# One wait between a batch's row stores, and the exponential of the memory weights moved behind the values' copies

## The chip, the cores and the metric

The kernel runs on one core of a Trainium2 chip. A core has five engines that run their own instruction streams and meet at semaphores: TensorE (PE, matrix products), VectorE (DVE), ScalarE (ACT), GpSimd (POOL) and SyncE (SP, which issues DMAs). The metric is the device time of one execution in microseconds (us), the median of several.

## The reference

A block of a network on 4 sequences of 1024 rows with 256 columns, in float32: a layer norm, then the sum of the input, an attention part and a part of experts.

```python
xn = layernorm(x)
x = x + attention(xn) + ffn(xn)

# attention, 16 heads of 16 columns, 4 memories
sq, sk = elu(q) + 1, elu(k) + 1
a_f, n_f = einsum(sq, memories), einsum(sq, memory_norms)
rel = n_f.mean(-1)                     # per batch and head: mean over the 1024 rows
w = softmax(rel, axis=0)               # over the 4 memories: the "memory weights"
out_fine = ((a_f / clip(n_f, EPS)) * w).sum(0)
memory_output = p * out_fine + (1 - p) * out_coarse      # p from a small gate network
local_output = causal_linear_attention(q, k, v)
attention = (gate * memory_output + (1 - gate) * local_output) @ w_o.T

# ffn: softmax over 8 experts, the best 2 of each row, plus a shared expert
g = silu(xn @ w_gate[e]) * (xn @ w_up[e]);  y += cw[row, e] * (g @ w_down[e])
y += silu(xn @ sw_gate) * (xn @ sw_up) @ sw_down
```

## The kernel before

The program has three phases, one after the other.

**Tokens phase** (the first 186 us or so). It is unrolled over the four batches, which the code counts as b = 2, 3, 4, 5, and two buffers u = 0, 1 alternate. For each batch DVE takes the mean and variance of the rows (meanvar, lines 572 and 577), POOL makes rstd and shift of them (varp, rstd, shift, lines 801 to 804, function scale_and_shift), ACT normalizes the rows into xn (line 447), PE transposes them in two halves (t_a, line 311), ACT and DVE copy the transposes as a high and a low part, xT (lines 463 and 669), and PE multiplies them with the shared expert's weights (t_g and t_u, and then the down product t_y; each product is three matmuls, lines 87 to 89). DVE adds t_y to the rows (xn_in, line 697), and SP stores that. Each batch is 8 tiles of 128 rows. From the logits DVE computes where each row goes, slot_i, and POOL then stores every row twice (TOP = 2), once for each chosen expert, to the place in d_rows: 16 indirect DMAs of 128 rows, 128 KB each (line 821). Each adds 16 to a semaphore s_sc[u] when it has landed. Around the end of a batch these stores run while PE does the down product of the second half, the transposes of the next batch's second half, and its first products. SP then loads the batch after that and a quarter of the experts' weights.

**Experts phase** (to about 360 us). SP loads blocks of 128 rows of one expert from d_rows, and PE, ACT and DVE run the experts on them.

**Attention phase** (the rest). All engines walk one list, ATT_ORDER, made by attention_order(); an item is (what, batch, tile, part), and each engine does those items that are its own, in the list's order, and waits on semaphores for the others'. So an item's place in the list sets its place in an engine's queue, even where its data are ready earlier or later. A batch has 8 tiles, t = 0 to 7. What matters here:

- "norms": PE multiplies sq with the memories; ACT copies it to with_mem (line 1554), four copies for a tile.
- "mean" (t = 0): PE gives the mean of n_f over the batch; DVE copies it to mw and subtracts the maximum (lines 1644 to 1648).
- "mexp" (t = 0): ACT takes the exponential of mw (line 1526).
- "weights": DVE sums and divides, five small instructions on mw (lines 1654 to 1661).
- "values": PE multiplies the masked scores (probs) with v (line 1452); ACT copies the result to valT, two copies (line 1574); PE multiplies these with a picking matrix in "local" (line 1474), and DVE divides (den, line 1687, to mem_rows, line 1690).
- "state" and "fold": the running sum of keys and values on PE (line 1497) and its copy on DVE (line 1712).
- "coef": DVE makes the coefficients from the gate's e_t, from rn and from mw (lines 1695 to 1698). It is the first reader of mw after "weights", in the list of the next tile.
- "scores": PE's scores (line 1417) and DVE's masking, probs (line 1681).

Of the kernel before, what the change touches and what calls it, by code (L numbers as in the profile page):

```python
# [36 lines left out]
TS = ST // P  # L37
# [72 lines left out]
def tokens_phase(nc, d, c, w):  # L110

    with ExitStack() as scope:
# [677 lines left out]
        def _(pool):  # L790
# [17 lines left out]
            for it in range(B // 2):  # L808
                for u in range(2):
                    b = it * 2 + (2 + u)  # L810
                    if b == 2:
                        scale_and_shift(3)

                    pool.wait_ge(s_slot, b + 1)
                    pool.wait_ge(c["s_load"], (c["n_load"] - 1) * 16)
                    pool.wait_ge(s_tick, b)
                    pool.tensor_tensor(tick_p[:, :], c["lane"][:, :], c["lane"][:, :],
                                       ALU.add).then_inc(s_tick, 1)
                    for t in range(NT):
                        for k in range(TOP):  # L820
                            pool.indirect_dma_start(  # L821
                                d["rows"], bass.IndirectOffsetOnAxis(ap=slot_i[u][:, k, t:t + 1], axis=0),
                                xn[u][:, t, :], None).then_inc(s_sc[u], 16)
                    if b < B:
                        scale_and_shift(b + 2)
# [270 lines left out]
def attention_order():  # L1096
    def parts(items, engine):
        return [(what + engine, *at) for what, *at in items if what in ON_TWO]
# [7 lines left out]
    for i, (b, t) in enumerate(tiles):  # L1106
# [16 lines left out]
        order += [("scores", b, t, j) for j in range(4)]  # L1123
        if i > 1:
            order.append(("outT", *tiles[i - 2], 0))
        if i:
            order += [("coef", *tiles[i - 1], 0), ("rest", *tiles[i - 1], 0)]
        order.append(("coarseT", b, t, 0))
# [12 lines left out]
        if i + 1 < len(tiles):  # L1141
            order += [("norms", *tiles[i + 1], j) for j in range(NB3)]
        if t == 0:
            order += [("mean", b, 0, 0), ("mexp", b, 0, 0)]
        order += ahead + [("values", b, t, 0), ("values", b, t, 1)] + behind + [("gate", b, t, 0)]
        projected = parts(ahead + behind, ".dve")
        rows = [x for x in projected if x[0] == "xT.dve"]
        late = [x for x in projected if x[0] != "xT.dve"]
        order += parts(ahead + behind, ".act")
        if t < NT - 1:  # L1150
            order.append(("state", b, t, 1))
        if t == 0:
            order.append(("weights", b, 0, 0))
        order += rows
        if t < NT - 1:
            order.append(("fold", b, t, 1))
# [24 lines left out]
def attention_phase(nc, d, c, w):  # L1181

    with ExitStack() as scope:
# [400 lines left out]
        def _(dve):  # L1584
# [17 lines left out]
            def walk(items):  # L1602
                link, _ = chain(dve, s_dve)
                for item in items:
# [45 lines left out]
                                          ALU.subtract).then_inc(s_mx, 1)  # L1650
                    elif what == "weights":

                        since(dve, s_mexp, b + 1)
                        link(dve.tensor_reduce(mw_m[:, 0, :, :], by_memory, AX.X, ALU.add))
                        link(dve.reciprocal(mw_m[:, 1, :, :], mw_m[:, 0, :, :]))
# [232 lines left out]
```

## Time and profile before

| | |
|---|---|
| median of 3 runs | 712.3 us |
| their lowest and highest | 708.75, 714.91 us |
| the profiled execution | 708.62 us |
| its span, first to last instruction | 706.7 us |
| mean granted TensorE clock | 0.956 of full speed |
| PE busy | 626.9 us (89%) |
| DVE busy | 509.9 us (72%) |
| ACT busy | 355.9 us (50%) |
| POOL busy | 313.4 us (44%) |

Busy times are sums over the span; an engine that is idle in one phase can be the one that all wait for in another. The profile was taken of one execution. An engine's row ends with the idle time just before it and what ended that, in square brackets; "issue" is a time for which the profile shows no wait, and "remote" one whose release it cannot match to an instruction. The ends of PE's instructions are modelled, and some of its records can be missing.

### The profile page before, as it was taken

To read this page: it belongs to the slowest core of one execution; us is meant where nothing else is said; L and a number is where in the kernel's file an instruction comes from. 1 tells how busy PE (TensorE), PEld (TensorE's weight loads), DVE (VectorE), ACT (ScalarE), POOL (GpSimd) and SP (SyncE) were. 2 spreads that over 40 slices of the span, in tenths; PEclk is the share of its full clock that TensorE was granted. 3 is DMA by queue.
4 is the path that set the end of the run, shared out by engine and by line. 5 is a ranking of instruction groups with operands and counts; after the bars stand their busy time and mean duration, and the time that the engine had idled before them with its cause. 6 is when DMAs were issued, how large, how long until landed. Compare 5 with 4: busy or idle time off the path is not lost. (4 is left out here: it accounts for less than half of the span.)

```text
span 706.7 us, 22451 instructions
## 1 busy us (share of the span) xinstructions
PE 626.9 (89%) x7874; PEld 520.5 (74%) x7874; DVE 509.9 (72%) x1362; ACT 355.9 (50%) x902; POOL 313.4 (44%) x406
## 2 busy tenths in 40 slices
PE   1997869699499999999968999989998999989885
PEld 0785748578399999999956777777776777777663
DVE  3674829358466666666656988889888788888886
ACT  4453625252434444444435766556565475646542
POOL 1153543707481000000030766656675566666775
PEclk9999989989599999999978999999999999999996
DMA  8128271534353333333350012221140202103120
GB/s 283 64 91 277 78 257 56 189 136 149 121 167 116 117 120 118 121 114 117 116 183 34 18 33 92 84 85 32 36 137 29 84 25 65 60 17 92 33 63 32
DMA packets 60123, 71.39 MB, mean 101 GB/s; under 512 B 7612, under 2 KB 55068, under 8 KB 60028
## 3 DMA queue, kind: packets, MB, share of 16 engines
q1 hardware_dynamic: 50956, 52.61, 22.9%
q0 software_dynamic: 6656, 16.86, 7.3%
q8 instruction: 67, 1.10, 0.7%
q10 hardware_dynamic: 2416, 0.59, 0.4%
q14 instruction: 28, 0.23, 0.1%
HBM read 38.45 MB, written 31.59 MB: 99 GB/s over the span
## 5 line engine op out<-in xcount | busy, mean ns | idle before, releaser
L1741 POOL TENSOR_TENSOR tick_a<-lane 128x1 f32<-128x1 f32 x32 | 6.3, 196 | 148.1 <-POOLq L834 145.8
L1744 POOL DMA_INDIRECT yg<-d_grouped_y,from_row x64 | 62.5, 977 | 15.5 <-issue 11.6
L978 ACT ACTIVATE hb<-e_h 88x256 fp32r<-88x256 f32 x72 | 27.5, 382 | 52.7 <-PE e_h L953 52.7
L87 PE MATMUL e_up<-wb,xb 128*128 x144 | 53.0, 368 | 0.5 <-issue 0.5
L1554 ACT ACTIVATE with_mem<-a_ring 128x340 f32<-128x340 f32 x128 | 47.0, 450 | 7.8 <-PE a_ring L1398 7.5
L1010 DVE TENSOR_TENSOR h_sb<-e_up,silu 128x176 f32<-128x176 f32 x72 | 24.6, 342 | 35.3 <-ACT silu L973 35.3
L87 PE MATMUL e_y<-wd,hb 88*128 x146 | 48.7, 334 | 1.0 <-DVE hb L1017 1.0
L1769 POOL TENSOR_TENSOR mem_rows<-mem_rows 128x512 f32<-128x512 f32 x16 | 24.3, 1518 | 54.5 <-DVE mem_rows L1721 54.5
L1681 DVE TENSOR_TENSOR probs<-a_ring,causal 128x256 f32<-128x256 f32 x128 | 45.1, 415 | 3.5 <-remote 3.3
L89 PE MATMUL e_up<-wb,xb 128*128 x144 | 46.9, 326 | 0.0
L88 PE MATMUL e_up<-wb,xb 128*128 x144 | 46.9, 326 | 0.0
L973 ACT ACTIVATE silu<-e_up 128x176 f32<-128x176 f32 x72 | 22.9, 318 | 41.1 <-PE e_up L89 41.1
L1474 PE MATMUL a_ring<-ident,valT 128*128 128x68 f32 x256 | 35.3, 279 | 8.4 <-ACT valT L1574 8.4
L88 PE MATMUL e_y<-wd,hb 88*128 x146 | 41.6, 285 | 0.0
L1474 PEld LDWEIGHTS a_ring<-ident,valT 128*128 128x128 f32 x256 | 31.0, 191 | 14.2 <-issue 11.0
L89 PE MATMUL e_y<-wd,hb 88*128 x146 | 41.3, 283 | 0.0
L1017 DVE TENSOR_TENSOR hb<-e_h,hb 88x256 fp32r<-88x256 f32 x72 | 30.3, 420 | 14.7 <-ACT hb L978 12.5
L821 POOL DMA_INDIRECT d_rows<-v,slot_i x32 | 34.0, 1063 | 9.5 <-issue 9.5
L821 POOL DMA_INDIRECT d_rows<-sqT,slot_i x32 | 33.0, 1032 | 9.5 <-issue 9.5
L1430 PE MATMUL a_ring<-wo,attT 128*128 128x256 f32 x128 | 35.2, 399 | 1.3 <-ACT attT L1563 1.1
L1571 ACT ACTIVATE hid<-a_ring,b 64x128 f32<-64x128 f32 x32 | 11.6, 364 | 48.6 <-PE a_ring L1440 36.8
L87 PE MATMUL t_g<-xT,shared_w 128*128 128x512 f32 (+1 forms) x48 | 22.1, 461 | 15.6 <-issue 15.6
(300 smaller groups left out, 2069.7 us busy)
## 6 DMA issues: line engine op xcount, KB each, us to landing
xg<-d_rows SPq DMA_DIRECT2D x77, 128.0 KB, 2.0
d_grouped_y<-y_sb SPq DMA_DIRECT2D x73, 128.0 KB, 1.8
d_base<-xn_in SPq DMA_DIRECT2D x8, 512.0 KB
xn_in<-d_xn SPq DMA_DIRECT2D x4, 1024.0 KB
total<-d_base SPq DMA_DIRECT2D x8, 512.0 KB
out<-total SPq DMA_DIRECT2D x7, 512.0 KB, 3.3
mem_rows<-in_w_up SPq DMA_DIRECT2D x4, 704.0 KB
v<-in_x_tok SPq DMA_DIRECT2D x2, 1024.0 KB
```

Of the source, the lines that this page charges most:

```text
L87: pe.matmul(out, a[0], b[0], start=start, stop=False)
L88: pe.matmul(out, a[0], b[1], start=False, stop=False)
L89: return pe.matmul(out, a[1], b[0], start=False, stop=stop)
L821: pool.indirect_dma_start(d["rows"], bass.IndirectOffsetOnAxis(ap=slot_i[u][:, k, t:t + 1], axis=0), xn[u][:, t, :], None).then_inc(s_sc[u ...
L978: act.activation(hb[o][0][:, :, :], ps_h[o][0:FC, 0:2 * P].rearrange("p (k n) -> p k n", k=2), ACT.Copy).then_inc(s_hh, 1)
L1010: dve.tensor_tensor(h_sb[q][:, :], ps_up[q][:, F:2 * F], silu[q][:, :], ALU.mult).then_inc(s_h, 1)
L1017: dve.tensor_tensor(hb[o][1][:, :, :], ps_h[o][0:FC, 0:2 * P].rearrange("p (k n) -> p k n", k=2), hb[o][0][:, :, :].bitcast(F32), ALU.subt ...
L1430: mm = pe.matmul(ps[:, 0:H], attT[t % 2][:, m, :], c["wo"][:, m, :], start=(m == 0), stop=(m == KC - 1))
L1474: mm = pe.matmul(ps[:, 0:NH * HE].rearrange("p (m g n) -> p m g n", m=KC, g=PP)[:, :, g, :], valT[:, g, :], pick.rearrange("p (m r) e -> p ...
L1554: act.activation(with_mem[((b - 1) * NT + t) % 3][:, j:NP:PP, :], ps[:, 0:KC * WN].rearrange("p (m w) -> p m w", m=KC), ACT.Copy).then_inc ...
L1681: dve.tensor_tensor(probs[:, j, :, :], ps[:, 0:4 * CH].rearrange("p (h i) -> p h i", i=CH), c["causal"][:, 0:CH].unsqueeze(1).broadcast_to ...
L1744: pool.indirect_dma_start(yg[tile % GATHERS][:, k, :], None, d["grouped_y"], bass.IndirectOffsetOnAxis(ap=c["from"][:, k, tile:tile + 1], ...
```

## The change

It has two parts that do not touch each other.

POOL, between the eighth and the ninth of the 16 row stores of a batch (TS = 4 of the 8 tiles, TOP = 2 stores each), waits until the first eight have landed. This is done in three of the four batches, not in the last. The instruction stream of POOL before, from a batch's tick to the next batch's (tick_p is a tiny instruction ahead of the stores):

```order
L817 TENSOR_TENSOR tick_p<-lane 128x1 [waits t_tick,c_load,t_slot]
L821 DMA d_rows<-sqT,slot_i 33792x256 x16
L801 TENSOR_TENSOR varp<-meanvar,ln_eps 128x8 [waits t_mv]
L802 TENSOR_TENSOR rstd<-varp,half_neg 128x8 [waits t_pool]
L803 TENSOR_TENSOR shift<-meanvar,neg 128x8 [waits t_pool]
L804 TENSOR_TENSOR shift<-shift,rstd 128x8 [waits t_pool]
```

And in the changed kernel:

```order
L817 TENSOR_TENSOR tick_p<-lane 128x1 [waits t_tick,c_load,t_slot]
L823 DMA d_rows<-sqT,slot_i 33792x256 x8
L823 DMA d_rows<-sqT,slot_i 33792x256 [waits t_sc0]
L823 DMA d_rows<-sqT,slot_i 33792x256 x7
L801 TENSOR_TENSOR varp<-meanvar,ln_eps 128x8 [waits t_mv]
L802 TENSOR_TENSOR rstd<-varp,half_neg 128x8 [waits t_pool]
```

The ninth store has got a wait for t_sc0, the landing of the first eight, and all behind it on POOL stands behind that wait too.

In the attention phase the item "mexp" moves from before the values of tile 0 to behind its gate, and "weights" from the end of tile 0 into tile 1, just ahead of "coef". ACT's instructions at tile 0 of the first batch, before:

```order
L1554 ACTIVATE with_mem<-a_ring 128x2x170 [waits a_ps_norms] x4
L1526 ACTIVATE mw<-mw 128x64 [waits a_mx]
L1574 ACTIVATE valT<-a_ring 128x4x64 [waits a_ps_values] x2
L1550 ACTIVATE v<-a_ring 128x16x16 [waits a_ps_v]
L1578 ACTIVATE e_t<-a_ring,half_b 128x1 [waits a_ps_gate]
L1567 ACTIVATE coarseT<-a_ring 128x256 [waits a_ps_hidden,a_ps_coarseT]
```

And in the changed kernel (its lines are numbered four higher there):

```order
L1558 ACTIVATE with_mem<-a_ring 128x2x170 [waits a_ps_norms] x4
L1578 ACTIVATE valT<-a_ring 128x4x64 [waits a_ps_values] x2
L1554 ACTIVATE v<-a_ring 128x16x16 [waits a_ps_v]
L1582 ACTIVATE e_t<-a_ring,half_b 128x1 [waits a_ps_gate]
L1530 ACTIVATE mw<-mw 128x64 [waits a_mx]
L1571 ACTIVATE coarseT<-a_ring 128x256 [waits a_ps_hidden,a_ps_coarseT]
```

The exponential, mw from mw, has moved behind valT, v and e_t. DVE's instructions from the end of "mean" to "coef" of tile 0 (a_ps_... are PE's signals, a_mexp is ACT's exponential), before:

```order
L1648 TENSOR_TENSOR mw<-mw,mw_m 128x64 [waits a_dve]
L1654 TENSOR_REDUCE mw_m<-mw 128x16 [waits a_mexp]
L1655 RECIPROCAL mw_m<-mw_m 128x16 [waits a_dve]
L1656 TENSOR_TENSOR mw_m<-mw_m,half_gate 128x16 [waits a_dve]
L1658 TENSOR_TENSOR mw<-mw,mw_m 128x64 [waits a_dve]
L1661 TENSOR_TENSOR mw<-mw,alive 128x64 [waits a_dve]
L1712 TENSOR_TENSOR state<-a_sums,same_head 128x272 [waits a_ps_state,a_dve]
L1687 SCALAR_TENSOR_TENSOR den<-a_ring,over_keep 128x16 [waits a_ps_local]
L1689 RECIPROCAL den<-den 128x16 [waits a_dve]
L1690 TENSOR_TENSOR mem_rows<-a_ring,den 128x256 [waits a_dve]
L1681 TENSOR_TENSOR probs<-a_ring,causal 128x256 [waits a_ps_values,a_ps_scores] x4
L1695 TENSOR_SCALAR e_t<-e_t 128x1 [waits a_e]
```

And in the changed kernel:

```order
L1652 TENSOR_TENSOR mw<-mw,mw_m 128x64 [waits a_dve]
L1717 TENSOR_TENSOR state<-a_sums,same_head 128x272 [waits a_ps_state]
L1692 SCALAR_TENSOR_TENSOR den<-a_ring,over_keep 128x16 [waits a_ps_local]
L1694 RECIPROCAL den<-den 128x16 [waits a_dve]
L1695 TENSOR_TENSOR mem_rows<-a_ring,den 128x256 [waits a_dve]
L1686 TENSOR_TENSOR probs<-a_ring,causal 128x256 [waits a_ps_values,a_ps_scores] x4
L1659 TENSOR_REDUCE mw_m<-mw 128x16 [waits a_mexp]
L1660 RECIPROCAL mw_m<-mw_m 128x16 [waits a_dve]
L1661 TENSOR_TENSOR mw_m<-mw_m,half_gate 128x16 [waits a_dve]
L1663 TENSOR_TENSOR mw<-mw,mw_m 128x64 [waits a_dve]
L1666 TENSOR_TENSOR mw<-mw,alive 128x64 [waits a_dve]
L1700 TENSOR_SCALAR e_t<-e_t 128x1 [waits a_e,a_dve]
```

The five instructions of the weights have moved from before the fold of the state to behind the four probs of the next tile. PE's and SP's streams have the same instructions in the same order as before. The diff:

```diff
@@ -817,6 +817,8 @@
                     for t in range(NT):
+                        if t == TS and b <= B:
+                            pool.wait_ge(s_sc[u], it * SCATTERED + 16 * TOP * TS)
                         for k in range(TOP):
                             pool.indirect_dma_start(
...
@@ -1123,6 +1125,8 @@
         if i > 1:
             order.append(("outT", *tiles[i - 2], 0))
+        if t == 1:
+            order.append(("weights", b, 0, 0))
         if i:
             order += [("coef", *tiles[i - 1], 0), ("rest", *tiles[i - 1], 0)]
...
         if t == 0:
-            order += [("mean", b, 0, 0), ("mexp", b, 0, 0)]
+            order.append(("mean", b, 0, 0))
         order += ahead + [("values", b, t, 0), ("values", b, t, 1)] + behind + [("gate", b, t, 0)]
+        if t == 0:
+            order.append(("mexp", b, 0, 0))
...
-        if t == 0:
-            order.append(("weights", b, 0, 0))
         order += rows
...
@@ -1650,6 +1654,7 @@
                     elif what == "weights":
 
+                        by_memory = mw[:, :, :, :].rearrange("p g n r -> p g r n")
                         since(dve, s_mexp, b + 1)
```

## Rows read from the trace of the kernel before

**Rows 1.** The page: busy time of the engines, and the granted clock in 40 slices.

```profile
PE 626.9 (89%) x7874; PEld 520.5 (74%) x7874; DVE 509.9 (72%) x1362; ACT 355.9 (50%) x902; POOL 313.4 (44%) x406
...
PEclk9999989989599999999978999999999999999996
```

**Rows 2.** Busy time by stretch: three of the tokens phase, one of the attention phase.

```profile
core 0: us, PE busy (x) PEld busy (x) DVE busy (x) ACT busy (x) POOL busy (x), PEclk, DMA share, GB/s
60.00:90.00 30.00, 27.77 (x163) 23.14 (x164) 21.51 (x60) 16.15 (x29) 13.19 (x16) 0.94 0.50 175
90.00:130.00 40.00, 31.70 (x183) 25.80 (x182) 23.30 (x62) 17.35 (x31) 18.54 (x21) 0.91 0.46 162
130.00:170.00 40.00, 33.17 (x188) 26.93 (x187) 21.47 (x56) 15.22 (x26) 16.71 (x17) 0.91 0.45 153
460.00:540.00 80.00, 76.62 (x1468) 60.01 (x1467) 69.11 (x178) 50.80 (x135) 52.04 (x63) 1.00 0.21 66
```

**Rows 3.** Waits from 36 to 185 us: who, for whom, total, times, longest.

```profile
ACT xT L463 <- remote: 27.8, 6, 7.7
POOL varp L801 <- DVE meanvar L577: 19.7, 2, 11.1
...
PE t_g L87 <- issue: 15.6, 3, 6.7
...
DVE xn_in L697 <- remote: 11.6, 3, 3.9
```

**Rows 4.** Timeline at one batch's end: start, duration, instruction, idle before.

```profile
50.74 0.69 DVE L697 TENSOR_TENSOR xn_in<-t_y,skT 128x512 f32<-128x512 f32 x1 [1.30 <-issue]
55.31 0.69 DVE L697 TENSOR_TENSOR xn_in<-t_y,skT 128x512 f32<-128x512 f32 x1 [3.88 <-remote]
...
52.58 0.28 PE L89 MATMUL t_y<-shared_w,hT 96*128 96x256 f32 x1
52.69 1.04 PE L311 MATMUL t_a<-ident,v 128*128 128x128 f32 x8
...
60.27 0.49 PE L87 MATMUL t_g<-xT,shared_w 128*104 128x512 f32 x1 [3.75 <-issue]
...
56.72 0.60 ACT L463 ACTIVATE xT<-t_a 128x512 fp32r<-128x512 f32 x1 [6.26 <-remote]
```

**Rows 5.** POOL's timeline there: the eighth, ninth and sixteenth row store.

```profile
50.65 0.96 POOL L821 DMA_INDIRECT d_rows<-sqT,slot_i  x1 [0.30 <-issue]
51.92 0.96 POOL L821 DMA_INDIRECT d_rows<-sqT,slot_i  x1 [0.30 <-issue]
...
60.78 0.96 POOL L821 DMA_INDIRECT d_rows<-sqT,slot_i  x1 [0.30 <-issue]
```

**Rows 6.** The page's DMA issues: count, KB each, median us to landing.

```profile
d_grouped_y<-y_sb SPq DMA_DIRECT2D x73, 128.0 KB, 1.8
```

**Rows 7.** ACT at a batch's first tile, and the exponential's wait over the attention phase.

```profile
459.45 1.49 ACT L1554 ACTIVATE with_mem<-a_ring 128x340 f32<-128x340 f32 x4 [0.63 <-PE a_ring L1398]
463.41 0.26 ACT L1526 ACTIVATE mw<-mw 128x64 f32<-128x64 f32 x1 [2.47 <-DVE mw L1648]
463.57 0.64 ACT L1574 ACTIVATE valT<-a_ring 128x256 f32<-128x256 f32 x2
...
ACT mw L1526 <- DVE mw L1648: 9.4, 4, 2.5
```

**Rows 8.** PE's timeline at the same tile.

```profile
460.20 0.86 PE L1452 MATMUL a_ring<-probs,v 64*32 64x64 f32 x64
...
462.20 0.33 PE L1497 MATMUL a_sums<-v,k_tok 64*32 64x34 f32 x16
464.36 1.08 PE L1474 MATMUL a_ring<-ident,valT 128*128 128x68 f32 x8 [1.82 <-ACT valT L1574]
```

**Rows 9.** DVE's timeline at the same tile and the start of the next.

```profile
463.70 0.22 DVE L1654 TENSOR_REDUCE mw_m<-mw 128x16 f32<-128x64 f32 x1 [0.32 <-ACT mw L1526]
...
464.97 0.44 DVE L1712 TENSOR_TENSOR state<-a_sums,same_head 128x272 f32<-128x272 f32 x1
...
466.92 1.41 DVE L1681 TENSOR_TENSOR probs<-a_ring,causal 128x256 f32<-128x256 f32 x4
468.24 0.15 DVE L1695 TENSOR_SCALAR e_t<-e_t 128x1 f32<-128x1 f32 x1
```

## The prediction

> **What bounds the kernel now.** I first read the page's busy shares and the clock row [rows 1]: TensorE is busy for 627 of 706.7 us, and its clock (a slice is 17.7 us) is below full speed in some early slices, in the middle and at the end. The table of stretches shows what lies there [rows 2]. In the attention stage (460 to 540) PE is busy for 76.6 of 80 us at full clock and DVE for 69.1: PE bounds it, with DVE close behind. In the tokens stage PE is busy for 27.8 of 30, 31.7 of 40 and 33.2 of 40 us, at a mean clock of 0.94, 0.91 and 0.91. There something makes PE wait, and this is the stage in which POOL stores rows.
>
> The list of waits of the tokens stage names it [rows 3]. PE waits three times before the first product of the second half (t_g, line 87), 15.6 us in all, the longest 6.7. ACT waits six times before the copy xT (line 463), 27.8 us, "remote", and DVE three times before xn_in (line 697), 11.6 us, "remote". On a kernel of one core "remote" means only that the page has no near finished instruction that explains the release. All of these follow PE's results. Around 52 us it can be followed: the last product that line 697 waits for begins at 52.58 and should be done at 52.86, and DVE starts only at 55.31; the transposes are recorded from 52.69 to 53.73, and ACT starts on the first at 56.72 [rows 4]. So PE's signals come 2.4 and over 3 us late, ACT and DVE stand idle, and PE, which needs their xT, begins t_g at 60.27 after 3.75 us. POOL meanwhile issues its 16 row stores, one each 1.27 us: the eighth starts at 50.65, the ninth at 51.92, the last ends at 61.7 [rows 5]. The signal of the product before the eighth store's end was in time (DVE started at 50.74 without a named wait [rows 4]); those after the ninth store has started are late. The pauses end shortly after the train of stores does.
>
> **Part 1: POOL's wait.** It is added three times (b = 2, 3, 4; not in the last batch). The ninth store may start when the eighth has landed. What the pause costs POOL: the trace shows no landing for these stores. The nearest row is that of another 128 KB store to HBM, from SP, with 1.8 us from issue to landing [rows 6]. Counted from the eighth's start it lands at 52.5, 0.5 us after the ninth started; counted from the end of its issue (50.65 + 0.96 = 51.61) at 53.4, 1.5 us after. I take 1.0 us, the middle. Queued behind on POOL are eight stores and then varp, rstd and shift for the batch after next. Varp waits for DVE's meanvar twice, 19.7 us in all and 11.1 at the longest, so 8.6 at the shortest [rows 3]: a POOL that is 1.0 us late is hidden with 7 us to spare. Of the others, ACT waits for this batch's stores only in the next batch (before it overwrites xn), and DVE one pass later, before it overwrites slot_i. So by the trace, the instruction alone costs 0, and its upper bound, if its 1.5 us were all on the path, is 3 x 1.5 = 4.5 us.
>
> What it could bring is another matter: if a pause with everything landed clears what delays PE's signals, up to 15.6 us of PE's waits go, and the half clock that follows each of them. That clock costs (1 - 0.94) x 30 + (1 - 0.91) x 40 x 2 = 9.0 us [rows 2]. The other end is a loss: the late signals seem to end with the train of stores, and a train that ends 1.0 us later would hold them 1.0 us longer, 3 us in all. So the range of this part is -24.6 to +4.5. I take 0, since the same lateness begins in all three trains at the same step of the program (the second half of the down product), so the trace cannot tell the ninth store from that step.
>
> The Trainium skill speaks against a gain here: "DMA: Bandwidth & Descriptors", section "Queues, rings and completion order", says that each DMA engine takes turns between the rings that have work, a packet at a time. By that, holding stores back gives SP's loads little that they don't have, and the same bytes move: the sum stays at this part's 0. The same page (section "Anatomy of one DMA") gives a fixed cost of about 2 us for any DMA up to its semaphore, most of it the receipt of the write; as an estimate by the page the pause would be nearer 1.7 us than 1.0, which the 7 us of cover still hide.
>
> **Part 2: the exponential behind the values' copies.** At the first tile of each batch ACT finishes with_mem at 460.94 (459.45 + 1.49), idles 2.47 us for DVE's mean, does the exponential at 463.41, and only then the two values' copies valT, 463.57 to 464.21 [rows 7]. The values themselves were done on PE at 461.06 (460.20 + 0.86), and PE stands idle for 1.82 us until it may multiply valT at 464.36 [rows 8]. With the exponential behind them, the copies run from 461.06 to 461.7, and PE goes on right behind its state product, which ends at 462.53: 1.82 us earlier. There are four such places; ACT's wait before the exponential is 9.4 us over four [rows 7], so they are alike.
>
> DVE gains less. Its five weights instructions stand from 463.70 to 464.97 before the fold [rows 9]; they move, all 1.27 us of them, to behind the next tile's four probs. The local result is done, and probs begins, at 466.92; 1.82 earlier is 465.10. From there to e_t it was 1.32 us (466.92 to 468.24), now 1.32 + 1.27: e_t at 467.69 where it was 468.24, 0.55 earlier. The exponential's own 0.26 us on ACT falls where ACT waits for the next coarseT; the fold of the state moves 1.27 up, which only helps. So each batch gains between 0.55 us (if DVE is the bound) and 1.82 (if PE is). PE is the busier of the two, 76.6 against 69.1, and I take 1.1, the middle: 4 x 1.1 = 4.4 us, bounds 2.2 and 7.3. On the other side, if PE came no earlier (the state or a bank late instead), the weights would put their 1.27 before the coefficients for nothing: +5.1 us.
>
> **The sum.** 0 - 4.4 = -4.4 us. The profiled execution took 708.6 us (span 706.7 and 1.9 around it), which is at the fast end of the runs of before (708.75 to 714.91, median 712.3). On its own time 704.2; on the median 707.9, so 708 us.
>
> **The rivals.** *The pause clears the signals.* Price: at most 15.6 + 9.0 us; I take two thirds, 16, since the copies' own hand-overs (ACT 0.6, DVE 0.7, twice) remain, and since the stage's loads then come due sooner. 712.3 - 4.4 - 16 = 692 us. For it: in all three trains the signals of the first eight stores come in time, and PE, ACT and DVE have nothing else to wait for. Against it: the coincidence of step named above, and that part of the lateness (ACT's at 56.72 and later) falls in the stretch in which the next batch's big loads move as well, which the pause doesn't touch.
> *It clears a part*, for example the first 2.4 us of lateness of each batch (DVE's, and what follows) and not that under SP's loads: about 3 x 2.4 = 7 us, 701 us.
> *The change doesn't do what it says*: the eighth store has landed before the ninth could start anyway. Then part 1 is an exact 0 and the time is the forecast's 708; the same number, so it shares the forecast's chance. By the skill's taking of turns the time is this one too.
> *Slower.* The late signals are let go by the end of the train of stores; the pause moves that end by 1.0 to 1.5 us in three batches, 3 to 4.5 us, and the move of the weights hits DVE's coefficients, +5.1: 712.3 + 4 + 5 = 721 us. It decides if the pause is over about 1 us and DVE, not PE, is last at the tile's end. With one half of it alone, 715.
>
> **How the numbers follow.** Forecast (708, from 705 to 712) 0.43; signals cleared (692, 685 to 698) 0.25; in part (701, 698 to 705) 0.17; slower (712 to 721) 0.15. The runs of before lie 0.9% apart, so under about 1% a measurement of this kernel cannot tell a change from none: the bounds are 705.2 and 719.4. Faster: 0.25 + 0.17 + a little of the forecast's lower edge = 0.45. Slower: 0.07, half of the last case. Same: 0.48. The range of 8 in 10 has to reach into the case of cleared signals: 689 to 716, which leaves out its lowest third and the upper half of the slow case. The forecast's own range is 705 to 712.
>
> **What the profile after would show.** Part 1: between the eighth and the ninth store a gap of about 1.3 us in place of 0.3, released by a DMA, three times; varp's wait about 1 us shorter. If PE's wait before t_g stays near 15.6 us and line 463's near 27.8, the forecast's zero is right; if they fall below half, the rival is. If the longest of them grows by 1 us each, the slow one is. Part 2: valT's copies right behind with_mem, no 1.8 us of idle before PE's product of valT at the first tile of a batch, and the weights' five instructions between probs and e_t. I would be wrong if DVE's coefficients at tile 1 come later than before.

## The result: 5% faster, 30 us beyond the forecast

The changed kernel takes 678.15 us (median, 677.32 to 679.28), the kernel before took 711.22 in the same set of runs (708.75 to 714.91): ratio 0.9532, 95% interval 0.9485 to 0.9579. The forecast was 708, its range 689 to 716, so the time lies below the range. Medians are over all runs of a kernel, while ratios and their intervals leave out runs of a slower state at a lower clock, four of the seven of the kernel before on chip 9 and three of the seven on chip 6, and so show smaller gains there than the medians do. The profiled execution took 677.7 us (span 675.8) against 708.6 (span 706.7): 30.9 us less of span. POOL's first gather, which opens the attention stage, starts at 340.9 us in place of 363.0. So 22.1 us are gone before the attention stage and 8.8 in it.

The page of the changed kernel, with busy times and the granted clock, answers to [rows 1]:

```profile
PE 615.6 (91%) x7874; PEld 513.7 (76%) x7874; DVE 510.0 (75%) x1362; ACT 355.8 (53%) x902; POOL 313.3 (46%) x406
...
PEclk9999999998799999999979999999999999999996
```

PE does the same 7874 multiplications in 11.3 us less busy time: none is missing, and its mean clock was higher (0.976 against 0.956). By stretches, as in [rows 2]:

```profile
core 0: us, PE busy (x) PEld busy (x) DVE busy (x) ACT busy (x) POOL busy (x), PEclk, DMA share, GB/s
60.00:90.00 30.00, 27.58 (x171) 23.34 (x172) 22.62 (x61) 15.29 (x28) 16.88 (x20) 1.00 0.53 191
90.00:130.00 40.00, 37.53 (x223) 30.75 (x223) 24.72 (x64) 19.12 (x35) 23.55 (x26) 1.00 0.63 222
130.00:170.00 40.00, 28.85 (x177) 24.34 (x175) 31.03 (x90) 17.91 (x33) 20.72 (x22) 0.91 0.40 147
460.00:540.00 80.00, 78.04 (x1486) 61.15 (x1486) 70.94 (x185) 51.06 (x137) 52.72 (x64) 1.00 0.22 68
```

Between 90 and 130 us PE does 223 multiplications where it did 183, at full clock in place of 0.91. From 130 to 170 us the changed kernel is already further on in the program, so that this row doesn't compare like with like. The list of waits from 36 to 185 us, as [rows 3]:

```profile
ACT xT L463 <- PE t_a L311: 8.6, 3, 2.9
...
DVE xn_in L697 <- PE t_y L89: 8.3, 6, 1.5
ACT silu L477 <- remote: 8.0, 3, 2.7
...
POOL d_rows L823 <- DMA d_rows<-sqT,slot_i: 3.4, 2, 1.7
...
POOL varp L801 <- issue: 2.6, 2, 1.5
...
POOL d_rows L823 <- DMA d_rows<-v,slot_i: 1.7, 1, 1.7
```

No row for PE before t_g is left (15.6 us before), ACT's wait before xT fell from 27.8 to 8.6 us, and what the copies and xn_in wait for is now named: PE's own instruction, not "remote". Not all of the lateness is gone: ACT waits 2.7 us, "remote", before line 477's silu in each of the three batches. New are POOL's three waits for a landing. The timeline at the first batch's end, as [rows 4, 5]:

```profile
50.55 0.69 DVE L697 TENSOR_TENSOR xn_in<-t_y,skT 128x512 f32<-128x512 f32 x1 [1.29 <-PE t_y L89]
52.50 1.04 PE L311 MATMUL t_a<-ident,v 128*128 128x128 f32 x8
52.70 0.69 DVE L697 TENSOR_TENSOR xn_in<-t_y,skT 128x512 f32<-128x512 f32 x1 [1.46 <-PE t_y L89]
53.14 1.09 ACT L463 ACTIVATE xT<-t_a 128x512 fp32r<-128x512 f32 x2 [2.87 <-PE t_a L311]
56.16 0.40 PE L87 MATMUL t_g<-xT,shared_w 128*104 128x512 f32 x1
...
50.47 0.96 POOL L823 DMA_INDIRECT d_rows<-sqT,slot_i  x1 [0.30 <-issue]
53.10 0.96 POOL L823 DMA_INDIRECT d_rows<-sqT,slot_i  x1 [1.67 <-DMA d_rows<-sqT,slot_i]
```

DVE starts at 52.70, 0.04 us after the product that it waits for (52.38 + 0.28), where it was 2.4 us late. ACT starts at 53.14 where it was 56.72, and does both copies in a row. PE's products of the first half, recorded from 53.29 (53.49 before), lead without a stop into the t_g of the second half at 56.16, where PE stood idle from 56.5 to 60.27 before. POOL's eighth store ends at 51.43 and the ninth starts 1.67 us later, 1.37 more than without the wait.

In the attention stage, at the first tile of a batch (ACT, PE, then DVE in the next tile), as [rows 7 to 9]:

```profile
436.08 1.49 ACT L1558 ACTIVATE with_mem<-a_ring 128x340 f32<-128x340 f32 x4 [0.63 <-PE a_ring L1402]
437.64 0.66 ACT L1578 ACTIVATE valT<-a_ring 128x256 f32<-128x256 f32 x2
440.03 0.26 ACT L1530 ACTIVATE mw<-mw 128x64 f32<-128x64 f32 x1 [0.85 <-DVE mw L1652]
...
438.81 0.33 PE L1501 MATMUL a_sums<-v,k_tok 64*32 64x34 f32 x16
439.07 1.11 PE L1478 MATMUL a_ring<-ident,valT 128*128 128x68 f32 x8
...
442.99 0.21 DVE L1659 TENSOR_REDUCE mw_m<-mw 128x16 f32<-128x64 f32 x1
```

The copies stand behind with_mem, and PE goes from the state product to valT with no idle time, where it stood for 1.82 us. PE's whole wait before valT was, and is now:

```profile
PE a_ring L1474 <- ACT valT L1574: 8.4, 8, 1.8
```
```profile
PE a_ring L1478 <- ACT valT L1578: 1.2, 4, 0.3
```

### The profile page after: what moved, and what is told of

The parts are those of the page before. It is cut to its first block and busy times, and to the rows that moved or that the text cites. A ratio compares the mean times of both kernels' runs of the same rounds, so it can differ in the third digit from the quotient of the medians.

```text
span 675.8 us, 22454 instructions
## 1 busy us (share of the span) xinstructions
PE 615.6 (91%) x7874; PEld 513.7 (76%) x7874; DVE 510.0 (75%) x1362; ACT 355.8 (53%) x902; POOL 313.3 (46%) x406
## 5 line engine op out<-in xcount | busy, mean ns | idle before, releaser
L1012 DVE TENSOR_TENSOR h_sb<-e_up,silu 128x176 f32<-128x176 f32 x72 | 24.6, 342 | 36.0 <-ACT silu L975 36.0
L1774 POOL TENSOR_TENSOR prod<-prod 128x512 f32<-128x512 f32 x16 | 21.5, 1345 | 31.8 <-DVE prod L1726 31.8
```

Of the source, the lines that this page charges most:

```text
L1774: link(pool.tensor_tensor(part[:, :, :, :], prod[:, :, 0:2, :], prod[:, :, 2:4, :], ALU.add))
```

## The experiments

Each set of runs was on one chip, beside the kernel before on the same chip. The set of a run matters here, so they stand by chip; the chips are told apart by their numbers.

| chip | kernel before, us | kernel | us (median) | ratio, 95% interval |
|---|---|---|---|---|
| (first) | 711.2 | changed kernel | 678.2 | 0.953 (0.949 to 0.958) |
| 9 | 715.1 | wait alone (e1) | 694.0 | 0.978 (0.960 to 0.995) |
| 9 | | order alone (e2) | 700.8 | 0.989 (0.967 to 1.011) |
| 9 | | POOL work in place of the wait, gap 1.6 us (e3) | 680.3 | 0.960 (0.944 to 0.976) |
| 9 | | wait ahead of the 5th store (e4) | 697.1 | 0.983 (0.966 to 1.000) |
| 15 | 682.0 | wait ahead of the 13th store (e5) | 668.4 | 0.982 (0.979 to 0.985) |
| 15 | | wait in the last batch too (e6) | 668.2 | 0.981 (0.978 to 0.984) |
| 15 | | three waits a train (e7) | 679.7 | 0.995 (0.993 to 0.998) |
| 15 | | no wait, memsets between the stores (e8) | 668.7 | 0.981 (0.978 to 0.984) |
| 5 | 682.4 | order alone (e9) | 668.7 | 0.980 (0.977 to 0.983) |
| 5 | | wait alone (e10) | 682.3 | 1.000 (0.998 to 1.002) |
| 5 | | wait ahead of the 13th store (e11) | 668.3 | 0.978 (0.976 to 0.981) |
| 5 | | POOL work, gap 0.9 us (e12) | 669.4 | 0.978 (0.974 to 0.983) |
| 13 | 713.8 | wait and exponential (e13) | 685.6 | 0.961 (0.957 to 0.966) |
| 13 | | wait and weights (e14) | 696.9 | 0.973 (0.966 to 0.980) |
| 13 | | POOL work, gap 0.9 us (e15) | 687.6 | 0.964 (0.960 to 0.968) |
| 6 | 714.5 | wait and exponential (e16) | 687.7 | 0.966 (0.958 to 0.975) |
| 6 | | wait in the last batch too (e17) | 678.3 | 0.953 (0.944 to 0.961) |
| 5 | 682.9 | wait ahead of the 13th store (e18) | 667.9 | 0.978 (0.975 to 0.980) |

**The two halves.** e1 is the kernel before with the wait, e2 the changed kernel without it:

```diff
 for t in range(NT):
+    if t == TS and b <= B:
+        pool.wait_ge(s_sc[u], it * SCATTERED + 16 * TOP * TS)
     for k in range(TOP):
```

> The kernel before with POOL's three waits and nothing of the new order. The changed kernel is 33 us faster: 20 us of that lie between the first and the last slot_i of the tokens stage, some 22 us ahead of the first expert, and 8.8 us in the attention stage. Theory A (the wait stops PE's signals from coming late, and that is worth 20 to 24 us): ratio 0.965 to 0.970, 686 to 690 us, and PE's 15.6 us of waits before t_g gone. Rival (the prediction's step: the lateness goes with the step of the program, the wait is worth 0): 708 to 711 us, with the waits before t_g as they were.

> The changed kernel without the three waits: only the exponential and the weights moved in the attention stage. Theory A: everything ahead of the attention stage is as before, and the attention stage is 7 to 9 us shorter, so 702 to 705 us (ratio 0.987 to 0.991). If part of the attention stage's 8.8 us came from the earlier stages (another state of the clock at its start), 705 to 708. Rival (the order is the whole gain): 678 us.

Against the kernel before the set on chip 9 is imprecise: its seven runs there spread from 704.5 to 719.1 us, and the interval of the order alone takes in 1. The four kernels of the set can be compared with one another. With a break and the old order (e1) it is 694.0 us, with the new order and no break (e2) 700.8, with both (e3, below) 680.3. So a break is worth 20.5 us and the order 13.7. With the order alone the first gather stood about where it was in the kernel before (361.0 us, 363.0), with the wait alone at 342.0. The list of waits of e2 shows PE's waits before t_g whole (10.4 + 6.6 us), that of e1 has none:

```profile
PE t_g L87 <- DVE xT L669: 10.4, 2, 5.2
...
PE t_g L87 <- issue: 6.6, 1, 6.6
```

So the wait does bring PE's signals in time for the second half, and my zero for it is refuted for this chip. The order is worth three times the 4.4 us that I took.

**A break without a landing.** e3:

```diff
-                            pool.wait_ge(s_sc[u], it * SCATTERED + 16 * TOP * TS)
+                            pool.tensor_tensor(gap[:, b - 2, :], ln_eps[:, 0:6], half_neg[:, 0:6], ALU.pow)
```

> The changed kernel, with the wait for the landing replaced by work of POOL: one power over 128 x 6 elements, which should take 1.3 to 1.7 us, so that the gap between the eighth and the ninth store is about as long as with the wait, but nothing asks whether the first eight have landed (by then they probably have). Theory B (any break of that length in the train of stores clears the signals): 678 to 682 us, t_g's waits gone. Rival (it is the wait on the landing itself that matters, since it holds the ninth store until the queue is empty): 700 to 704 us, with the late signals as before. A landing that takes 1.67 us and a gap of 1.5 are hard to tell apart, so only the second outcome would decide.

The POOL timeline of e3 (eighth store, the power, ninth store):

```profile
50.05 0.96 POOL L824 DMA_INDIRECT d_rows<-sqT,slot_i  x1 [0.30 <-issue]
51.04 1.36 POOL L822 TENSOR_TENSOR gap<-ln_eps,half_neg 128x6 f32<-128x6 f32 x1
52.60 1.04 POOL L824 DMA_INDIRECT d_rows<-sqT,slot_i  x1 [0.19 <-issue]
```

680.3 us, 20.5 below the order alone on the same chip: a gap of 1.59 us (51.01 to 52.60) in which POOL issues no store does what the wait does. Nothing has to ask for the landing. Whether the eight had landed by then all the same is not told apart, as the expectation says.

**Where the pause stands.** e4 has the wait at t == 2, ahead of the fifth store:

```diff
-                        if t == TS and b <= B:
-                            pool.wait_ge(s_sc[u], it * SCATTERED + 16 * TOP * TS)
+                        if t == 2 and b <= B:
+                            pool.wait_ge(s_sc[u], it * SCATTERED + 16 * TOP * 2)
```

> The changed kernel with the wait moved forward: POOL waits for the landing of the first four stores ahead of the fifth, and twelve then follow in a row. Theory D (a count: PE's signals come late once about eight stores have been issued without a pause): signals are in time up to the twelfth store and late from the thirteenth on, so about a third to a half of the gain is kept: 685 to 695 us, and the first waits of PE appear 5 us later in a train than before. Theory C (the lateness belongs to a step of the program at which the ninth store stood): late from the ninth store's time on, as before the change: 700 to 704 us. Theory E (one pause anywhere in a train is enough): 678 to 682 us.

697.1 us, 3.7 below no wait, which the runs of the two kernels (694.95 to 698.85 and 697.89 to 706.53) don't part clearly. Its trace settles the coincidence on which my zero stood. Its timeline on DVE, ACT and again ACT:

```profile
52.86 0.69 DVE L697 TENSOR_TENSOR xn_in<-t_y,skT 128x512 f32<-128x512 f32 x1 [1.45 <-PE t_y L89]
53.30 0.60 ACT L463 ACTIVATE xT<-t_a 128x512 fp32r<-128x512 f32 x1 [2.87 <-issue]
...
64.38 0.59 ACT L477 ACTIVATE silu<-t_g 96x512 f32<-96x512 f32 x1 [5.93 <-remote]
```

The steps that were late in the kernel before (line 697, then 463) are in time, and those behind them, line 477's silu, are late by up to 6 us (11.9 us in two "remote" waits): the product that this silu waits for was done at 58.1, and the row of twelve ends at 63.0. In this stage the lateness belongs to a row of POOL's stores that has become long, not to a step of the program. It isn't a plain count: it began at the ninth store in a row of sixteen, and here the second xT already waits 1.16 us at the sixth of twelve, though its transposes were all done at 53.70.

**The other chip.** e5 to e8 were to try places and lengths further:

```diff
e5   if t == 6 and b <= B:     pool.wait_ge(s_sc[u], it * SCATTERED + 16 * TOP * 6)
e6   if t == TS:               (the changed kernel's wait, in all four batches)
e7   if t in (2, 4, 6):        pool.wait_ge(s_sc[u], it * SCATTERED + 16 * TOP * t)
e8   no wait; after each store: pool.memset(gap[:, one column], 0.0)
```

> The changed kernel with the wait moved back: POOL waits for the landing of the first twelve stores ahead of the thirteenth. Wait alone gave 694, order alone 701, a pause ahead of the fifth store 697 us, so hardly anything of the pause's gain is left when twelve stores follow it. If what counts is the longest row of stores without a pause (twelve here too): 694 to 700 us, with PE's signals late from the ninth to the twelfth store and in time after it. If what counts is that the pause comes soon after the signals begin to be late (it lets them go): 683 to 690 us, with a wait of PE that ends at the pause.

> The changed kernel with the wait in the last batch as well. In the changed kernel ACT still waits 8.6 us once (hf, line 548) during the last train, and the clock is half for 13.7 us behind it. If the pause works there as in the other trains: 3 to 8 us less, 670 to 675 us. If nothing but POOL's own end stands behind the last train (the tables of the experts wait for it): 678 to 680 us.

> The changed kernel with three pauses a train, ahead of the fifth, ninth and thirteenth store, in all four batches. If the lateness grows with the row of stores (1.5 to 2.9 us are left of it behind eight stores), rows of four clear the rest, which is worth 1 to 2 us a batch; but each pause moves POOL's last store by 1.4 us, so POOL ends 2.8 us later in a train, and its scale and shift for the batch after next, which now waits for nothing, come 2.8 us later: between 672 us (the first) and 685 us (the second).

> The changed kernel with no wait; instead one small memset of POOL between every two stores of the first three trains, 0.1 us of work and about as much around it, so that POOL gives up 1.5 to 3 us over a train, as much as the pause or more, but never over 0.6 us in a row. If PE's signals need one uninterrupted break of POOL: as with the order alone, 698 to 703 us, with t_g's waits as before. If they need only that POOL's stores come more slowly (one each 1.45 us instead of 1.27): 678 to 684 us.

They ran on a chip on which the kernel before takes 682 us. e5, e6 and e8 came to the same 668.2 to 668.7, and no trace of the four has a late signal, e8's neither, whose train is as without a wait: the 0.12 us of each memset fell into the 0.30 us between two stores, and the stores kept their 1.27 us. So these four say nothing of the late signals, and both halves ran again:

> The order alone once more. The last four kernels ran on another chip than the first four, and there the kernel before took 682 us, not 712 to 715, and none of their traces shows PE's signals late, that with twelve stores in a row and the one without any pause included. Theory F (on some chips the signals come late under the stores and on others not, whatever the kernel): on a chip where the kernel before takes about 682 us, the order alone gives 668 us, as all three kernels of the last set that have the order, and its trace has no wait before t_g; on one where it takes 710 to 715, it gives 698 to 703 with the waits of 15 us. Rival (the waits or memsets of those kernels were what cleared the signals): 680 to 682 us where the kernel before takes 682.

> The wait alone once more. Theory F: on a chip where the kernel before takes about 682 us the wait is worth nothing, 681 to 685 us (it even costs POOL 1.4 us a train); on one where it takes 710 to 715, 690 to 696 us as before. Rival: faster than the kernel before on both.

On chip 5 the wait alone is worth nothing (1.0002, interval 0.9981 to 1.0023) and the order alone 13.7 us. e9 is the same program as e2, with sixteen stores in a row. Its timeline at the place of [rows 4, 5], DVE and ACT, with the wait list's rows for both:

```profile
52.91 0.69 DVE L697 TENSOR_TENSOR xn_in<-t_y,skT 128x512 f32<-128x512 f32 x1 [1.46 <-PE t_y L89]
53.35 1.09 ACT L463 ACTIVATE xT<-t_a 128x512 fp32r<-128x512 f32 x2 [2.88 <-PE t_a L311]
...
ACT xT L463 <- PE t_a L311: 8.6, 3, 2.9
DVE xn_in L697 <- PE t_y L89: 8.3, 6, 1.5
```

These are the changed kernel's numbers (8.6, 8.3) without any pause. Theory F holds: on chips 9, 13, 6 and the first one, PE's signals come late under a long row of POOL's stores and the kernel before takes 711 to 715 us; on 5 and 15 they don't and it takes 682. The wait takes back on the former about two thirds of what the latter never lose: the wait alone leaves 694.0 us on chip 9 against 682.3 on chip 5, and the kernel with the wait in all four batches, below, takes 678.3 us on chip 6 against 668.2 on chip 15 (e17, e6, the same program). Of the 9.4 us between the spans of these two, 2.5 lie before the first gather (340.0 and 337.5 us) and 7 in the attention stage, where no run has a break. There, too, signals come late on such a chip. ACT's waits in that stage of the changed kernel:

```profile
ACT hid L1575 <- remote: 11.5, 4, 3.2
ACT coarseT L1571 <- remote: 4.7, 1, 4.7
```

None of the runs on chips 5 and 15 has a "remote" wait in the tokens or the attention stage. The four before hid (line 1575, a step of the small gate network) stand beside only two gathers of POOL each; at one of them PE's product is done at 642.85, the gathers are issued from 641.69 to 643.97, and ACT starts at 644.46, 1.6 us late.

e7 shows what waits cost there: 11.4 us more than e6. Its third pause lasts 5.7 us (SP's loads move as well, from 58 to 66 us 353 GB/s and a DMA share of 1.0; in the last batch the wait behind the twelfth store took 2.1). POOL's last store ends at 71.2 us, not 62.9, and the next batch waits for POOL's shift:

```profile
POOL d_rows L823 <- DMA d_rows<-sqT,slot_i: 5.7, 1, 5.7
```
```profile
ACT v L447 <- POOL shift L804: 2.9, 1, 2.9
ACT sqT L447 <- POOL shift L804: 2.8, 1, 2.8
```

In e5 the last store ends at 67.7, and e5 takes no longer than e6. So POOL's cover in this train is at least 4.8 us and, if ACT's waits for the shift are what e7 loses, less than 8.3.

> The wait ahead of the thirteenth store once more. On a chip without late signals it is 668 us, as it was. On one with them: 694 to 700 us if the longest row of stores counts, 683 to 690 us if the pause only has to come soon after the signals begin to be late. The landing that it waits for took 6 to 8 us on the other chip, so POOL's scale and shift come late for the next batch; that alone could cost 3 us a batch.

> The wait ahead of the thirteenth store, for a chip with late signals, which the two chips that it ran on weren't. There, from rows of eight stores (changed kernel, 678 us), of twelve behind four (697 us) and of sixteen (701 us): if the longest row of stores counts, 694 to 700 us; if the pause only has to come before the next batch's first products wait (t_g, 6.7 us after the ninth store of the kernel before), 683 to 690 us, with the wait of t_g cut short by the pause. On a chip without late signals: 668 us.

Both met chip 5: 668.3 and 667.9 us, as without a pause. What a wait ahead of the thirteenth store does on a chip with late signals is not known.

**How long a break.** The power over 128 x 2 elements in place of 128 x 6:

> The changed kernel with the wait replaced by a power over 128 x 2 elements, some 0.7 us of POOL's work, so that the gap between the eighth and the ninth store is about 0.9 us in place of 1.6 (and of 0.3 without). On a chip with late signals: 680 us if a break of 0.9 is as good as the one of 1.6 (which gave 680.3), near 690 if its worth goes with its length, 700 if it needs the landing or over 1 us. On a chip without: 668 us.

> The short break of 0.9 us in place of the wait, once more, since the last chip showed no late signals. On a chip where the kernel before takes 710 us or more: 680 us if 0.9 us is as good as 1.6, near 690 if its worth goes with its length, 700 if it is not enough. On one where it takes 682: 669 us again.

Chip 5 gave 669.4 us, chip 13 687.6. On chip 13 the gap was 0.95 us (50.67 to 51.62):

```profile
49.71 0.96 POOL L824 DMA_INDIRECT d_rows<-sqT,slot_i  x1 [0.30 <-issue]
50.70 0.73 POOL L822 TENSOR_TENSOR gap<-ln_eps,half_neg 128x2 f32<-128x2 f32 x1
51.62 1.04 POOL L824 DMA_INDIRECT d_rows<-sqT,slot_i  x1 [0.19 <-issue]
```

Its first gather stands at 346.5 us, between 361.0 (no break, e2) and 342.7 (1.59 us, e3): a break of 0.9 us brings some four fifths of the stage's gain, 14.5 of 18.3 us. The two were not on the same chip, the ratios' intervals overlap, and the profiled run (683.8 us) was the fastest of five, so this is a tendency. In so far as it holds, it speaks against the landing as what counts: 0.95 us is less than the 1.67 that a landing took in the changed kernel.

**The last train.**

> The wait in the last batch's train as well. On a chip with late signals: ACT's wait before hf (8.6 to 14 us in the last train) falls to the 7.0 and 3.4 us that it is on the chips without, and the time is 2 to 6 us under the changed kernel's 678: 672 to 676 us (ratio 0.945 to 0.950). If nothing hangs on it: 678 us (0.953). On a chip without: 668 us again.

678.3 us and 0.953, the changed kernel's ratio. ACT's waits before hf did become 7.0 and 3.4 us, but in the changed kernel they were no more than 8.6 and 2.8, and nothing hangs on the difference. No kernel tried beats the changed one on a chip with late signals by more than the measurement can tell. The changed kernel itself did not run on chips 5 and 15; e6 is the nearest to it there.

**The two halves of the order.** e13 and e16 put the weights back behind the first tile's projections; e14 leaves the exponential ahead of the copies. Both keep the wait:

```diff
e13  -        if t == 1:
     -            order.append(("weights", b, 0, 0))
     +        if t == 0:                                  (ahead of order += rows)
     +            order.append(("weights", b, 0, 0))
e14  -            order.append(("mean", b, 0, 0))
     +            order += [("mean", b, 0, 0), ("mexp", b, 0, 0)]
     -        if t == 0:                                  (behind gate)
     -            order.append(("mexp", b, 0, 0))
```

> The changed kernel with the weights back at their old place on DVE (behind the projections of the first tile), so that of the order only the exponential's move behind the values' copies stands. Two runs with the same chip's kernel before at 682.4 us gave 668.7 us for the order alone and 682.3 for the wait alone: the order is worth 13.7 us, not the 4.4 that I took. In their traces PE's idle time before it multiplies valT falls from 7.2 us to nothing, and four stretches of half clock behind it (3.4, 3.4, 6.8 and 3.4 us, which cost half their length, 8.5 us) are gone, with one or two microseconds of shorter half clock elsewhere. Theory G (the exponential's place is all of it: the idle time and the clock behind it): 668 to 670 us on a chip where the kernel before takes 682, ratio 0.979 to 0.983. Rival (DVE's weights at tile 0 keep DVE late, so PE waits elsewhere): 672 to 678 us, 0.986 to 0.993.

> The other half: the exponential as before, ahead of the values' copies, and only DVE's five weights instructions moved to the next tile. Theory G: 681 to 684 us on a chip where the kernel before takes 682 (ratio 0.998 to 1.003), with PE's 7.2 us of idle time before valT and four stretches of half clock there. Rival (DVE is what the stage waits for): 675 to 679 us. On a chip with late signals the kernel has the wait, so 690 to 696 us by theory G.

> The wait and the exponential's move without the weights' move. On the last chip, one with late signals (the kernel before took 713.8 us), the attention stage of the profiled runs took 340 us with it, against 350 with neither or the weights alone and 335 with both. Theory G' (the exponential's move takes PE's 7.2 us and the clock behind it; the weights' move then takes PE's waits for DVE's mem_rows, 5.2 us against 1.6): on a chip where the kernel before takes 682, 672 to 675 us, 4 to 6 more than with both. Rival (the weights' move is worth nothing, and the difference lay between chips): 668 to 670 us. On a chip with late signals: 685 us once more.

From the first gather to the end the profiled executions took 349.9 us with neither (e1), 350.7 with the weights (e14), 340.3 with the exponential (e13 and e16 both), 334.9 with both (the changed kernel). These are single profiles, of more than one chip, and they scatter: the kernel before, with neither too, took 343.7 in its profile, and e14's was taken of the slowest of four runs that lie 10 us apart. What e13 and e16 share is firmer: both lack the 1.8 us before valT and both have another wait in its place. By these numbers the weights' move is worth nothing by itself, and about 5 us behind the exponential's. One row of PE's waits, of e16 and of the changed kernel, shows a part of it:

```profile
PE a_ring L1410 <- DVE mem_rows L1695: 5.3, 7, 1.4
```
```profile
PE a_ring L1410 <- DVE mem_rows L1695: 1.6, 6, 0.4
```

In the kernel before it was 1.3 us. So moving the exponential alone makes DVE, with the weights still at their old place, late for PE, and moving the weights takes that back. On chip 6 the medians differ by 9.4 us (687.7 and e17's 678.3, which also has the fourth wait), more than these rows; the rest I can't place. Neither half ran on a chip without late signals.

**The clock behind the idle time.** e10 and e9 are the clean pair, one chip, no late signals. The attention stage from the first gather to the end, of e10 (old order), and three stretches of it, each of which holds most of one of PE's 1.8 us of idle time and what follows it:

```profile
337.30:679.70 342.40, 318.30 (x5908) 247.76 (x5906) 280.36 (x749) 203.94 (x535) 211.90 (x255) 0.95 0.20 61
437.00:447.00 10.00, 9.18 (x99) 7.38 (x100) 7.39 (x23) 5.14 (x15) 4.33 (x7) 0.83 0.19 60
519.00:531.00 12.00, 10.19 (x97) 8.10 (x98) 7.61 (x26) 4.71 (x14) 5.03 (x7) 0.72 0.11 33
604.00:614.00 10.00, 8.65 (x97) 6.84 (x98) 7.20 (x24) 4.73 (x14) 4.57 (x7) 0.83 0.13 40
```

and the stage of e9 (new order), whose clock in the same three stretches is 1.00:

```profile
338.30:666.90 328.60, 311.24 (x5910) 241.66 (x5908) 280.77 (x749) 204.24 (x535) 211.96 (x255) 0.98 0.21 64
```

The stage is 13.8 us shorter (342.4 and 328.6); the medians differ by 13.5 (682.3 and 668.7). For all but the same number of products PE is busy for 7.1 us less (318.3 and 311.2) and idle for 6.7 us less (24.1 and 17.4). The idle part is, but for small differences, the wait before valT, 7.2 us in e10 and no row in e9. The busy part is the clock: in e10 each 1.8 us of PE's idle time was followed by 3.4 to 6.8 us at the lower of the clock's two levels, 1.2 GHz (10 us at 0.83 are 3.4 us at half, 12 at 0.72 are 6.7), 17 us in sum behind the four. That need not follow: in the profile of the kernel before, with the same four places, only the one at 547 us was followed by such a stretch, of 3.4 us. So the same change gave 8.8 us in that pair of profiles and 13.8 in this one.

## Why the prediction was wrong

**The failed step** is in part 1: "I take 0, since the same lateness begins in all three trains at the same step of the program (the second half of the down product), so the trace cannot tell the ninth store from that step." What I read of the signals was right, and the measured term lies between the two ends (-24.6 and +4.5), but the value taken between them was not right. A coincidence that holds three times in a loop that repeats itself is one observation, and I let it decide. e4 parts the two, and e2 against e3, on one chip, measures the term: 20.5 us. On the profiled executions the stage before attention became 22.1 us shorter, close to the upper end of 24.6: PE's waits before t_g are gone whole. On chip 5 the term is 0, the value that I took, but that would have been luck: there the signals aren't late in the first place.

**The rival "the pause clears the signals"** had the mechanism and a wrong size. I took two thirds of 24.6, 16 us, for copies that would still cost their hand-overs and for loads that come due sooner; no run separates these. And it inherited the 4.4 us of part 2. With the terms as measured on chip 9 it reads 711.2 - 20.5 - 13.7 = 677 us, against 678.

**The pause.** The gap between the eighth and the ninth store is 1.67 us in place of 0.30, so the ninth is 1.37 later; I took 1.0 with 0.5 and 1.5 as bounds. The Trainium skill's "DMA: Bandwidth & Descriptors", section "Anatomy of one DMA", gives about 2 us as the fixed cost of a DMA of GpSimd's. My estimate by it was 1.7 us for the same delay, 0.3 too much: the trace has 1.67 us from the end of the eighth store's issue to the landing, and 2.63 from its start (50.47 to 53.10). The pause costs nothing by itself: e10 shows it on a chip where it has nothing to clear.

**The rule that spoke against a gain**, in the section "Queues, rings and completion order" of the same page of the Trainium skill, is about data in the rings. On chip 5 the wait does as little as it would have; on the others what came late was no data but PE's signals, of which it says nothing.

**Part 2** failed in its size: -4.4 taken, 7.3 as bound, 13.7 measured on chips 5 and 9 (8.8 in the first pair of profiles). The copies, PE's missing idle time (four times 1.8) and the weights' new place came as worked out; with the weights moved too, PE, not DVE, was what the tile waited for, so all of the 1.8 counted, and the middle between the two was wrong. Missing was the half clock behind the idle time, about 7 us of PE's busy time. The profile of before could only hint at it, since its stretch from 460 to 540 us shows 1.00 [rows 2].

**Slower, and no effect.** The train's end did move by 1.2 us (62.9 against 61.7), and no wait of the changed kernel shows a cost of it. The slower rival's +5.1 for DVE's weights did not appear: DVE's e_t of the next tile starts 8.17 us after the tile's first with_mem copy (436.08 to 444.25), where it was 8.79 (459.45 to 468.24), 0.6 sooner, as the prediction's 0.55 had it. "In part" (701) fits no run of the changed kernel, though e4 shows what it would look like.

What stays open: why PE's signals come late on some chips and not on others. The same program (e2, e9) issues its stores at the same 1.27 us on both. That the lateness in the tokens stage hangs on POOL's row of stores, where it happens, is shown by putting in a break and moving it (e1, e3, e4). In the attention stage late signals stand beside gathers, but no run changed those. On what path a signal is held is not shown.

## What to carry to other kernels

If a profile shows consumers that start microseconds after PE's product is done, with "remote" as the reason, look at what GpSimd issues meanwhile. A break of 1.6 us in a row of sixteen indirect DMAs gave back 20 us on such a chip, and a wait of about that length cost nothing on one without. Cost an idle time of PE as the time itself plus what the clock can lose behind it; in e10 the second was as large as the first, in the profile of the kernel before far smaller. Before a change of this kind is judged, run both kernels on more than one chip.

## What was not expected of the hardware

- One and the same kernel takes 682 us on two chips (5 and 15) and 711 to 715 on three others (6, 9 and 13) and in the first set, whose chip is not recorded, where the runs on one chip lie 0.7 to 2.1% apart. The difference in the traces is when PE's signals arrive under GpSimd's indirect stores: 2.4 and over 3 us late where they were followed, with ACT idle for up to 7.8 us, or in time. About 10 us of the difference are left with the break in, 7 of them in the attention stage.
- Where they are late, a break of 1.59 us between the eighth and the ninth of sixteen stores clears PE's waits before t_g, though not ACT's of 2.7 us near the train's end, and one of 0.95, on another chip, most of it; four stores, a break and twelve more bring them back, 1.2 us at the sixth and up to 6 towards the end.
- A memset of 0.12 us fits between two indirect stores without moving them (e8).
- The wait for a landing took 1.75 us behind the fourth store (e4) and 1.67 behind the eighth (changed kernel), and 5.0 to 7.9 behind the twelfth in the first three batches (e5, e7), at a time when SP's loads move.
- PE's clock fell to its lower level behind idle times of 1.8 us in a stage in which PE was otherwise nearly always busy, behind all four of them in e10 and behind one of four in the kernel before.
